# Graph network on one core: edge counts summed two tiles at a time, with 16 of 98 weight blocks per tile turned by TensorE

## The reference, cut to what matters

```python
edge_index = jnp.stack([src, dst])                      # 206,250 edges, sorted by dst; 6,250 nodes of 128 features
h = relu(layernorm(x))
x = x + segment_sum(edge_weight[:, None] * (sigmoid(h @ W_gate + b) * (h @ W))[dst], src)   # L0
h = relu(layernorm(x)); x = x + segment_sum(h[src], dst) @ W1.T + b1                        # L1
h = relu(layernorm(x)); x = x + update(h, segment_sum(message(h[src], h[dst]), dst))        # L2
h = relu(layernorm(x)); x = x + relu(batchnorm(hypergraph(h, src, dst)))                    # L3
```

## Time and profile before

| what | value |
|---|---|
| median of 3 runs | 2562.01 us (2561.71 to 2567.41) |
| the profiled execution's own time | 2568.25 us |
| its span | 2566.4 us |
| PE busy in the span | 2309.7 us (90%) |
| DVE busy | 1596.8 us (62%) |
| ACT busy | 1181.9 us (46%) |
| stage A | 0 to about 119 us |
| stage B | about 119 to 1320 us |
| stage C | from about 1320 us |

### The profile page before, as it was taken

The page is one execution under the profiler, slowest core; times in us unless marked ns, Lnnn a source line. Parts: engine busy times, 40 slices in busy tenths (PEclk is TensorE's granted clock), DMA queues, the critical chain, the costliest instruction groups (busy, mean ns, idle before and its releaser), DMA issues.

```text
span 2566.4 us, 70830 instructions
## 1 busy us (share of the span) xinstructions
PE 2309.7 (90%) x27901; PEld 1990.4 (78%) x27901; DVE 1596.8 (62%) x3655; ACT 1181.9 (46%) x2490; POOL 46.3 (2%) x52
## 2 busy tenths in 40 slices
PE   3489999999899998999939999899998999999997
PEld 2368878887787887877838888788887888887886
DVE  8689999999999998999962333234333112122223
ACT  3488778877777876888831222122221000011112
POOL 3300000000000000000000000000000000000000
PEclk9599999999999998999979999999998999999998
DMA  7589999999999999999989999999997999999998
GB/s 197 119 166 220 208 209 210 219 210 207 209 186 221 207 203 193 204 218 214 217 197 228 290 289 290 262 260 259 257 258 204 290 289 290 273 245 244 261 266 193
DMA packets 1608984, 589.35 MB, mean 230 GB/s; under 512 B 964422, under 2 KB 1605450, under 8 KB 1608567
## 3 DMA queue, kind: packets, MB, share of 16 engines
q1 hardware_dynamic: 1604869, 579.88, 101.8%
q0 software_dynamic: 1600, 4.92, 0.7%
q10 hardware_dynamic: 2226, 0.62, 0.2%
HBM read 255.26 MB, written 89.20 MB: 134 GB/s over the span
## 4 chain that ended last, share of the span: by engine, by line
PE 49%; SPq 22%; DMA 11%; DVE 6%; issue 5%; ACT 5%; POOL 1%; DVEq 0%; ACTq 0%; POOLq 0%
PE ps L676 33%; SPq L419 13%; SPq L446 8%; DMA counts_by_source<-stage 7%; PE ps L589 2%; ACT stage L1208 2%; PE ps L591 2%; PE ps L590 2%; ACT stage L1193 2%; DVE X L924 2%; PE ps L614 2%; DMA a_turned<-counts_by_source 2%; PE ps L615 2%; PE ps L616 2%; PE ps L597 1%
## 5 line engine op out<-in xcount | busy, mean ns | idle before, releaser
L1208 ACT CAST stage<-ps 128x784 f16<-128x784 f32 x784 | 655.7, 836 | 105.5 <-DMA counts_by_source<-stage 73.3
L676 PE MATMUL ps<-Ha,a_tiles 128*128 128x258 f16 x4606 | 523.8, 273 | 6.9 <-DVE Ha L994 6.9
L614 PE MATMUL ps<-hot_c,hot_r 128*128 128x98 f16 x3136 | 508.2, 211 | 14.1 <-DVE hot_c L912 7.5
L676 PEld LDWEIGHTS ps<-Ha,a_tiles 128*128 128x128 f16 x4606 | 449.9, 98 | 73.4 <-DVE Ha L994 7.6
L615 PE MATMUL ps<-hot_c,hot_r 128*128 128x98 f16 x3136 | 502.1, 210 | 0.0
L616 PE MATMUL ps<-hot_c,hot_r 128*128 128x98 f16 x3136 | 500.4, 210 | 0.0
L589 PE MATMUL ps<-g_in,wt 128*128 128x128 f16 x2401 | 431.5, 222 | 38.1 <-DVE X L924 21.7
L1193 ACT CAST stage<-ps 128x392 f16<-128x392 f32 x784 | 398.3, 508 | 141.9 <-PE ps L597 141.9
L590 PE MATMUL ps<-g_in,wt 128*128 128x128 f16 x2401 | 429.7, 222 | 0.0
L591 PE MATMUL ps<-g_in,wt 128*128 128x128 f16 x2401 | 429.6, 222 | 0.0
L924 DVE SCALAR_TENSOR_TENSOR X<-ps,X 128x512 f32<-128x512 f32 (+1 forms) x637 | 392.1, 649 | 45.5 <-PE ps L591 45.3
(11 more groups left out here) (195 smaller groups left out, 2029.9 us busy)
## 6 DMA issues: line engine op xcount, KB each, us to landing
a_tiles<-counts_by_source SPq DMA_DIRECT2D x147, 1600.0 KB, 13.7
counts_by_source<-stage SPq DMA_DIRECT2D x49, 1600.0 KB, 8.1
gated_parts<-G SPq DMA_DIRECT2D x7, 448.0 KB, 3.6
g_in<-gated_parts SPq DMA_DIRECT2D x98, 32.0 KB, 3.1
out_x<-X SPq DMA_DIRECT2D x12, 256.0 KB
edge_table<-tab SPq DMA_DIRECT2D x1, 2448.0 KB, 10.4
wt<-stage SPq DMA_TRANSPOSE x98, 10.9
dst_run<-in_dst SPq DMA_DIRECT2D x1, 612.4 KB
```

What stands on the lines that cost most here:

```text
L614: mm(into(0), rows_, codes(0), start=v == 0, stop=True, skip_group_check=True)
L676: last = mm(ps[:, sum_bank(ph, j, c), 0:PARTS], a_slot(ph, c, i), moving[:, i], start=i == 0, stop=i == TILES - 1)
L1208: a.copy(stage[:, b, 0:2, 0:TILES, u * SET_COLS:(u + 1) * SET_COLS], of).then_inc(s("hi_done"), 1)
```

## The change

Five things are done at once.

1. **Two tiles per addition.** Tiles are taken in pairs (24 pairs and one single). `sum_four` adds the products of both tiles of a pair into a bank, 24 matmuls, and then DVE adds it to X: 13 additions a pair, 325 in all. The fours of a pair are spread over two tiles (`fours_at`): one four in each of steps 1 to 6 of an odd tile and in each of steps 0 to 6 of the next even tile, the last of a single block.
2. **16 of the 98 blocks of a tile turned by PE.** In steps 1, 3, 4 and 6 of a tile, PE turns four blocks of the tile before (`turn_blocks`) into the PSUM bank in which it then sums a four, and ACT copies them to `wt` (`take_turned`). The DMA transposes shrink from 49 blocks to 24 and 17, two instructions.
3. **Drain reordered.** The counts are stored between the high and the low turns. `wt` has six half buffers in place of two whole ones, `g_in` has four, and SP waits for other counts of `four_done`. What follows the last tile are the sums of pair 23 and of tile 48.
4. **Keys by way of HBM.** To make room, keys and weights of all groups are stored to HBM in stage A, and SP loads one group per pair of tiles into a ring of two (`meta`).
5. **Pass one's first loads moved.** Tiles 1, 2 and 0 of the counts are loaded as soon as their memory is free, and not after the last addition; `first_tiles` takes them in the order 1, 2, 0, 3.

The core of the diff:

```diff
+TURN_STEPS = (1, 3, 4, 6)
+TURN_BLOCKS = 4
+def fours_at(c, h):
+    if c % 2:
+        return range(h - 1, h) if 1 <= h <= FIRST else range(0)
+    return range(FIRST + h, FIRST + h + 1) if FIRST + h < FOURS else range(0)
...
 # SP, hand_on
-                    if later(j, 2):
-                        sp.wait_ge(s("four_done"), (j - 1) * FOURS)
...
+                    if b and later(j, 2):
+                        sp.wait_ge(s("four_done"), (pair - 1) * FOURS + FIRST)
+                    elif later(j, 4):
+                        sp.wait_ge(s("four_done"), (pair - 1) * FOURS)
...
+                    turn(0, "hi_done", f"hi_turned{b}")
+                    sp.dma_start(two_tiles(j), stage[:, b, 0:FULL].rearrange("p (i a) d -> p i (a d)", a=2)).then_inc(s(f"stored{b}"), 16)
+                    turn(1, "lo_done", f"lo_turned{b}")
...
 # PE
+                def turn_blocks(t, b, r, f, e):
+                    if not (isinstance(f, int) and f < 2):
+                        pe.wait_ge(s("added"), f - 1)
...
+                    for x in range(TURN_BLOCKS):
+                        last = tr(to[:, x * P:(x + 1) * P], stage[:, b, FULL + r // 2 * TILES + i + x], ident16[:])
+                    last.then_inc(s("pe_turned"), 1)
...
                     for h in range(TILE_HOTS):
                         pe.wait_ge(s("hot_ready"), j * TILE_HOTS + (h + 1))
                         half_windows(j, c % 2, c, 2 * h)
+                        if h in TURN_STEPS and later(j, 1):
+                            r, g = TURN_STEPS.index(h), fours_at(c, h)[0]
+                            turn_blocks(j - 1, 1 - c % 2, r, n * FOURS + g, (cp + g) % 2)
                         half_windows(j, c % 2, c, 2 * h + 1)
-                        if later(j, 2):
-                            sums(j - 2, c % 2, k * (SLOTS // 2) + c // 2, h)
+                        for g in fours_at(c, h):
+                            if not isinstance(n, int) or n >= 0:
...
+                                if h in TURN_STEPS:
+                                    pe.wait_ge(s("turned_out"), (j - 1) * 4 + TURN_STEPS.index(h) + 1)
+                                sum_four(n, cp, g)
...
 # ACT, after the high copy of half u
+                        if u % 2 == 0 and u // 2 in TURN_STEPS and later(j, 1):
+                            take_turned(j - 1, c - 1, TURN_STEPS.index(u // 2))
...
+                    act.wait_ge(s("pe_turned"), t * 4 + r + 1)
+                    a.copy(wt[:, home(c, 1), r // 2, at_:at_ + TURN_BLOCKS].rearrange("p i d -> p (i d)"),
+                           ps[:, 6 + e, 0:TURN_BLOCKS * P // 2].bitcast(F16)).then_inc(s("turned_out"), 1)
...
 # SP, after the last tile
+                for j in (1, 2):
+                    load_counts(1, j, j)
...
+                load_counts(1, 0, 0)
+                sp.wait_ge(s("added"), FOURS * GROUPS)
+                for j in (3, 4, 5):
+                    load_counts(1, j, j)
```

More of the change, by code:

```diff
@@ L60 @@
 FULL = TILES + TILES % 2
+PARTED = FULL + WEIGHTS * TILES
+FIRST = 6
+HALF_TILES = (range(0, 4 * FIRST), range(4 * FIRST, TILES))
+TURN_STEPS = (1, 3, 4, 6)
+TURN_BLOCKS = 4
+TURN_FIRST = TILES - 2 * TURN_BLOCKS
+BY_DMA = (HALF_TILES[0], range(HALF_TILES[1].start, TURN_FIRST))
+HOMES = (((0, 1), (2, 3)), ((4, 5), (0, 2)), ((1, 3), (4, 0)), ((5, 2), (1, 4)), ((3, 0), (5, 1)), ((2, 4), (3, 5)))
+KEYS = 2 * P
+GROUP_WORDS = KEYS + WEIGHTS * P
 SET_COLS = HALF * WD
@@ L86, in later, with turned_tiles, pair_of, home @@
     return not isinstance(j, int) or j >= n
-def summed_at(h):
-    return range(2 * h, min(2 * h + 2, FOURS))
+def fours_at(c, h):
+    if c % 2:
+        return range(h - 1, h) if 1 <= h <= FIRST else range(0)
+    return range(FIRST + h, FIRST + h + 1) if FIRST + h < FOURS else range(0)
+def turned_tiles(r):
+    first = TURN_FIRST + r % 2 * TURN_BLOCKS
+    return first, first - HALF_TILES[1].start
+def pair_of(k, c):
+    return k * (SLOTS // 2) + c // 2
+def home(c, half):
+    return HOMES[c // 2 % len(HOMES)][c % 2][half]
 def load_at(ph, c):
@@ L387, in _ @@
                 turn_keys(m)
+            sp.wait_ge(s("meta_stored"), 32)
+            for n in range(2):
+                sp.dma_start(meta[:, n], groups[n]).then_inc(s(f"meta_in{n}"), 16)
             store_gated(0)
@@ L422, in layers @@
-                tiles_loop(sp, hand_on, 0)
-                counts_stored(sp)
-                sp.wait_ge(s("added"), FOURS * TILES)
+                        sp.dma_start(g_in[:, c % 4, part], slab(g_dram, j)[:, part]).then_inc(s(f"g_loaded{b}"), 16)
+                        for half, tiles in enumerate(BY_DMA):
+                            first = FULL + a * TILES + tiles.start
+                            sp.dma_start_transpose(wt[:, home(c, half), a, 0:len(tiles)],
+                                                   stage[:, b, first:first + len(tiles)].rearrange("p i d -> p (i d)")).then_inc(s(turned), 16)
@@ L965, in split @@
                 def split():
-                    counts_stored(dve)
                     for c in range(SET):
@@ L1216, in layers @@
                         low_parts(0, TILES - 1, u)
+                    for r in range(len(TURN_STEPS)):
+                        take_turned(TILES - 1, TILES - 1, r)
                 def next_rows(ph, j, c):
```

209 lines of the change are left out of this document (139 added, 70 removed).

## The result

The changed kernel takes 2593.4 us (median of 4 runs, 2590.58 to 2595.33), the kernel before 2562.15 beside it (2561.71 to 2567.41). The ratio is 1.0117, with a 95% interval of 1.0101 to 1.0133: slower by 31 us. The prediction was 2583, in a range of 2485 to 2625.

The account below looks back on a forecast made before the run. DVE was taken to bound stage B, nearly half of the time. Terms +34.8 (stage B), +1, +2.5 and -17 (pass one) sum to +21.3: 2589.5 us on the profiled execution, 2583 for the median, range 2485 to 2625.

Parts of the forecast that it names:

- The forecast's case: Stage B: PE's sums wait for ACT's copy in turning steps, 24.3 us a tile against 23.08; chance 0.61, 0.47 of it slower.
- Late code: Stage B: code that comes late, after which PE is slow too, costs 20 us before the change and stays.
- Which engine is next: Stage B: DVE, at 19.5 us a tile, no longer bounds; PE (20.8) and ACT (19.6) wait for each other in turn.
- The turning step: Stage B, steps in which PE turns blocks: PE stands 0.59 us for ACT's copy, so the step lasts 3.61.
- The pair of tiles: Stage B: two tiles take 48.5 us; ACT late out of the two steps without sums adds some 0.1.
- Store waits: Stage B: ACT's waits on the store of counts at tile starts, at most 14 us, go.
- Transfers: Stage B, SP's queue: some 20 us a tile lie beside 24.3, costed at nothing more; 41 blocks' turns take 6.7.
- Start of stage B: Stage A's end: two stores of about 0.4 us before the last turn of weights, plus one small copy: +1 us.
- Tail and pass one: After the last tile, remaining sums and additions: +2.5 us; pass one starting with the first part of its rows: -17.
- The hidden stand: Stage B rival: ACT's copy is done when PE's second half is, 22.2 us a tile, total 2486; chance 0.21.
- The clock rival: Stage B rival: PE's granted clock falls to 0.88, 23.6 us of PE work a tile, total 2712; chance 0.09.
- Doubled additions as the pace (DVE stays): Stage B rival: an addition of two tiles' sums costs what two did, period near 23.1, total 2528; chance 0.03.

Follow-up runs that it names:

- e1: The changed kernel with ACT's copy of the turned blocks moved ahead of the high copy of the step's first half: 2523.82 us, ratio 0.9826 to the kernel before.
- e5: The changed kernel with DVE also copying the bank's two halves to an unread buffer before each addition: 2613.65 us, ratio 1.0183 to the kernel before.
- e2: e1 with PE's turns also put ahead of the step's first half: 2510.44 us, ratio 0.9775 to the kernel before.
- e3: The changed kernel with no block turned by PE, all 98 of a tile turned by transfers: 2561.33 us, ratio 0.9975 to the kernel before.
- e7: e2 with the weights' turn in stage A put ahead of the stores of keys: 2504.03 us, ratio 0.9755 to the kernel before.
- e4: The changed kernel with pass one's first loads put back behind the last addition: 2610.22 us, ratio 1.0168 to the kernel before.
- e12: e7 with two blocks a turn and the small load of g_in just ahead of the store of counts: 2557.01 us, ratio 0.9974 to the kernel before.

## Why the prediction was right, and where its sizes were off

The forecast's case came: slower, by the stand at the sums of turning steps, and 10 us from the predicted median. Some 6 of the 10 are no matter of the kernel: the profiled execution of the kernel before lay 6.2 over its median, that of the changed kernel 0.5. Set beside the sum of 2589.5 it is 2593.92, 4.4 more, and that closeness owes something to misses that cancel, as told under *Late code*.

*Which engine is next.* Right. DVE at 81% was predicted as some 80%. e1 shows the stand to be the cause by one moved instruction, and e5 shows that DVE has no part in the pace of the steady tiles.

*The turning step.* Predicted 3.61 with PE standing 0.59; measured 3.64 with 0.60. A copy of 512 elements moves ACT's end by 509.54 - 509.06 = 0.48, predicted 0.49; its row is 0.611 in the mean, predicted 0.6. Four turns take 508.27 - 508.05 = 0.22 to issue, 0.056 each, as taken. By the rule that the prediction cited from the Trainium skill, "VectorE: DVE Perf Modes", section "The three transpose paths" (390 ns for a block), the four would have taken 1.56, an estimate; the trace doesn't agree, neither by the spacing nor by the row of one turn, some 0.22. A plain step took 523.88 - 521.05 = 2.83 in PE's rows, predicted 2.80. PE's wait for ACT is 84.9 us in the whole trace, not the 110 I forecast: the stand was counted from where the next matmul could be issued, the row counts from the last one's end, 0.16 later in each step.

*The pair of tiles.* A size that was off. I wrote that ACT, late out of the two steps without sums, costs "some 0.1 more". In the first turning step behind them it costs 0.4:

```profile
530.59 0.34 PE L689 MATMUL ps<-stage,minus 128*128 128x392 f16 x1
531.55 0.38 PE L721 MATMUL ps<-ident,stage 128*128 128x128 f16 x4
...
533.29 0.23 PE L681 MATMUL ps<-g_in,wt 128*128 128x128 f16 x1 [0.47 <-ACT wt L1346]
534.64 0.33 PE L689 MATMUL ps<-stage,minus 128*128 128x392 f16 x1
```

534.64 - 530.59 = 4.05, in place of 3.61. A quiet pair is 49.1 us for the predicted 48.5.

*Store waits.* Gone, as predicted.

*Late code.* DVE stood twice, 10.5 us together (8.2 in the earlier trace rows), so the places stayed. What they cost did not: the term of 20 us was too high. These are the two long tiles of the changed kernel:

```profile
725.83 0.33 SPq L479 DMA_DIRECT2D g_in<-gated_parts  x1
...
755.57 0.33 SPq L479 DMA_DIRECT2D g_in<-gated_parts  x1
...
1025.33 0.33 SPq L479 DMA_DIRECT2D g_in<-gated_parts  x1
...
1054.13 0.33 SPq L479 DMA_DIRECT2D g_in<-gated_parts  x1
```

They take 29.74 and 28.80 where their neighbours take 24.60: 9.3 us too much. In the kernel before the same two took 29.95 and 32.99, 16.8 over 23.08. Stage B's +36.9 is close to the predicted +34.8 by luck: without these places tiles 3 to 48 take 11.6 us more than the 1117.8 of the prediction, tiles 1 and 2 take 1.2 more, and late code 10.7 less. Why late code costs less than before is left open.

*Transfers.* Costed at nothing, which held: 20.7 us of SP's queue under 24.6, "some 20" in the prediction. The step was right by its sum and wrong in its parts. A turn of 41 blocks was put at 6.7 us; the high one is 6.98, the low one, behind the store, 8.97, and a load there 3.49. The earlier trace rows had the sign of it: the load of 157.67, 1.6 us behind the start of the store of tile 0 (156.04), took 3.44. The sentence "were that cover gone, they would still be under 23" holds for the transfers that it speaks of: in e2, at 22.85 us a tile, the queue's rows add up to 20.6. With 98 blocks, of which it doesn't speak, the queue is the bound (e3).

*Start of stage B.* Predicted +1, measured +4.3 at DVE and +4.7 at the hand-over. I counted the last lot's stores and not those of the lots before it, which delay it too (e7).

*Tail and pass one.* Predicted +2.5 and -17, measured +2.2 and -16.0; e4 gives the early loads by themselves as 13.

*The rivals.* The hidden stand, 2486, was right in its mechanism and as a ceiling: moving the copy alone gave 2524 with 0.10 of the stand left, moving the turn as well 2510 without it. The clock rival fell: 1.00 in the quiet stretch. Doubled additions as the pace (DVE stays) fell with e5.

## What to carry to other kernels

When a bound engine is relieved, walk one step of the loop with the queues of the two next engines side by side before spending the gain: here a round trip between engines (TensorE turns, ScalarE copies, TensorE reads) cost 0.6 us a turning step, 0.5 of it because the copy stood behind an independent 0.81 us copy, and one moved instruction turned 1.2% slower into 1.7% faster. Put the producer of such a round trip a half step earlier than its user, and its middle instruction at the head of its engine's queue. Work moved off a queue of transfers should be as little as brings that queue just under the pace: 12 of 98 blocks were better than 16 (by 0.3%) and than 8 (by 1.3%).

## What the hardware showed that was not expected

- A large store (1600 KB) holds the issuing queue for what comes behind it, not for itself: some 0.6 us for the store in the changed kernel's tiles 3 to 48, then 3.5 to 5.4 for a 32 KB load that else takes 0.33, and 7.0 to 9.4 (7.9 in the mean) for a turn that else takes 6.8 in the mean. It passes: in the kernel before, where the load came 4.9 us or more behind the store's start, it took 0.33 to 0.39. Putting another instruction there does not avoid it (e12: 13.82).
- A wait of PE can cost twice. In e3 PE stands for ACT about once in a pair of tiles, for up to 4.3 us, and just behind one such stand the granted clock falls for a while to 1.2 GHz:

```profile
525.85 0.22 PE L704 MATMUL ps<-hot_c,hot_r 128*128 128x98 f16 x1 [2.50 <-ACT stage L1314]
...
526.48 0.28 PE L706 MATMUL ps<-hot_c,hot_r 128*128 128x98 f16 x1
```

The matmul of 0.21 takes 0.28 there, and in the stretch from 526 to 530 us the granted clock is 0.57; from 574 to 578, a pair of tiles later, it is 0.57 again, so I take this to follow each of the longer stands. In the changed kernel 0.6 us of standing in half of the steps left it at 1.00 from 400 to 600 us.
